# Cross-attention with 128 small heads: values of two head groups share a PSUM region, one copy and one pick per token tile, and the projections move to the stacks' bank

## The reference

```
q = Wq @ x + bq ; k = Wk @ c + bk ; v = Wv @ c + bv      # per batch entry, 128 x 256
q, k = rope(q), rope(k)                                  # first 4 channels of each head
scores = q k^T / sqrt(8) ; p = softmax(scores)           # 256 x 256 per head
out = p v ; result = Wo @ out + bo
x = x + tanh(gate) * result
```

## Time and profile before

| | us |
|---|---|
| median of 3 runs (lowest, highest) | 1466.29 (1465.21, 1469.73) |
| profiled execution, its own time | 1469.58 |
| its span | 1467.8 |
| span minus TensorE's busy time | 255.4 |
| this stage in the trace, from VectorE's first fill at 234.9 to the next stage's first transpose at 464.9 | 230 |

### The profile page before, as it was taken

One profiled execution on the slowest core, in us unless ns is written; L12 is line 12 of the kernel. 1 busy time (PEld: TensorE's weight loads), 2 busy tenths in 40 slices (PEclk: granted clock), 3 DMA queues, 4 the chain that ended last, 5 costly groups with the idle time before them and its releaser, 6 DMA issues.

```text
span 1467.8 us, 23344 instructions
## 1 busy us (share of the span) xinstructions
PE 1212.4 (83%) x8571; PEld 854.7 (58%) x8571; DVE 870.8 (59%) x1864; ACT 608.3 (41%) x1335; POOL 332.1 (23%) x261
## 2 busy tenths in 40 slices
PE   1573683888897399889999977999977999999986
PEld 1353462434344156578988744555546788888854
DVE  6677795677766465325555576333355676566476
ACT  2442341456553241235433332333323665565443
POOL 1312000111000200213121124454420332223222
PEclk9655796789887599999999989999997999999998
DMA  7100005200001311500000051111011000000010
GB/s 246 55 2 2 0 1 216 121 1 2 1 1 73 111 62 37 188 22 2 1 1 1 1 189 33 55 43 54 21 62 59 1 1 1 1 1 1 1 44 29
DMA packets 32162, 63.93 MB, mean 44 GB/s; under 512 B 5344, under 2 KB 23392, under 8 KB 30144
## 3 DMA queue, kind: packets, MB, share of 16 engines
q1 hardware_dynamic: 31296, 60.52, 11.7%
q0 software_dynamic: 768, 2.10, 0.4%
HBM read 54.88 MB, written 9.70 MB: 44 GB/s over the span
## 4 chain that ended last, share of the span: by engine, by line
PE 55%; DVE 15%; issue 12%; POOL 4%; ACT 3%; DMA 1%; DVEq 0%; SPq 0%; POOLq 0%; ACTq 0%
PE psum L1436 7%; PE psum L2494 4%; PE psum L2522 4%; PE psum L2484 4%; PE psum L1418 3%; PE psum L1742 3%; PE psum L2466 2%; PE psum L2448 2%; PE psum L1077 2%; PE psum L2820 2%; PE psum L2046 2%; PE psum L1103 2%; PE psum L1760 2%; PE psum L1045 1%; PE psum L1110 1%
## 5 line engine op out<-in xcount | busy, mean ns | idle before, releaser
L1169 ACT ACTIVATE c_probs<-psum 128x512 f32<-128x512 f32 x128 | 76.3, 598 | 67.2 <-PE psum L1088 67.2
L1273 DVE TENSOR_REDUCE c_max<-psum 128x2 f32<-128x512 f32 x128 | 84.5, 687 | 29.6 <-PE psum L1077 23.1
L1479 ACT ACTIVATE m_h_hi<-m_h 128x512 bf16<-128x512 f32 x50 | 31.5, 629 | 143.1 <-DVE m_h L1521 123.0
L1544 POOL TENSOR_TENSOR m_h_lo<-m_h,m_h_hi 128x512 bf16<-128x512 f32 x50 | 61.4, 1228 | 111.1 <-ACT m_h_hi L1479 111.0
L1436 PE MATMUL psum<-ctxT_yT_hi,m_w_hi 128*128 128x512 bf16 x200 | 78.0, 390 | 6.0 <-DVE m_h L1495 6.0
L1436 PE MATMUL psum<-ctxT_yT_hi,m_w_lo 128*128 128x512 bf16 x200 | 78.0, 390 | 0.0
L1516 DVE TENSOR_TENSOR m_silu_up<-psum,m_silu 128x512 f32<-128x512 f32 x44 | 30.4, 692 | 80.0 <-PE psum L1436 79.7
L1436 PE MATMUL psum<-ctxT_yT_lo,m_w_hi 128*128 128x512 bf16 x200 | 77.6, 388 | 0.0
L2522 PE MATMUL psum<-a_wo,a_outT 128*128 128x256 f32 x256 | 75.1, 405 | 0.7 <-DVE x_tok L2703 0.7
L2143 PE MATMUL psum<-a_wo,a_outT 128*128 128x256 f32 x256 | 75.2, 407 | 0.0
L1286 POOL TENSOR_TENSOR c_rope_terms<-c_rope_terms 128x256 f32<-128x256 f32 x16 | 11.7, 728 | 257.6 <-DVE c_rope_terms L1229 257.6
(11 more groups left out here) (495 smaller groups left out, 3474.3 us busy)
## 6 DMA issues: line engine op xcount, KB each, us to landing
m_w<-m_w SPq DMA_DIRECT2D x8, 1536.0 KB, 16.7
m_w<-m_w SPq DMA_DIRECT2D x27, 384.0 KB, 3.1
a_wq<-a_wq SPq DMA_DIRECT2D x2, 2048.0 KB
a_wo<-a_wo SPq DMA_DIRECT2D x2, 2048.0 KB, 12.0
a_trig<-trig_sin_cos SPq DMA_DIRECT2D x1, 2048.0 KB, 6.3
ctxT_yT_hi<-f_gate_up SPq DMA_DIRECT2D x2, 1024.0 KB, 7.4
a_sin_cos<-a_trig SPq DMA_DIRECT2D x1, 2048.0 KB, 9.7
m_rows<-m_zeros SPq DMA_DIRECT2D x1, 1920.0 KB, 13.4
```

Source lines behind the costliest of these rows:

```text
L1169: e.activation(c1P[:, n % 8, :, :], ps[:, 2 + n % 2, :].rearrange("p (k t) -> p k t", k=2), ACT.Exp, scale=float(1.0 / np.sqrt(np.float32( ...
L1273: e.tensor_reduce(c1M[:, u % 2, j, :], ps[:, c1_score_bank(n), :].rearrange("p (q t) -> p q t", q=2), AX.X, ALU.max).then_inc(c1_mx, 1)
L1544: e.tensor_tensor(hl[:, n_ % hb, :], hf[:, n_ % hb, :], hh[:, n_ % hb, :], ALU.subtract).then_inc(s_hl, 1)
```

## The change

For each pair of groups of a tile, values now accumulate into one PSUM region: head slots of one group have their 8 value columns at 0 to 7 and ones at 8 to 15, those of the other at 16 to 23 and 24 to 31, and zeros elsewhere. The order of groups within a tile becomes 0, 2, 1, 3, so that the two groups of a region have heads in different halves. A tile thus needs two regions of 256 columns, which fill bank 4, one ScalarE copy of 512 columns (r = 8 of the next tile), and one job of picks (r = 11), now eight matmuls, four for the numerators and four for the sums, both into bank 7. The four `sums` matmuls per tile and their counters are gone, with three of the four copies.

ScalarE then copies the picked rows (512 columns, `rows`), VectorE inverts the sums out of SBUF in two halves (r = 12 and 13), and the multiplication goes to GpSimd (`normalise`). The output projection moves from r = 14 to r = 3 of the next tile; ScalarE applies gate and bias to it (`gated`), and GpSimd adds it to `x` (`residual`). VectorE has neither any more.

The projections move to bank 6, which they share with the stacks, and to r = 4, 8 and 12. They have counters of their own (`c1_jobs_full`, `c1_jobs_read`). A job in bank 6 waits for the copy of the last stack, and a stack waits for the read of the last job. Bank 7 keeps the maxima, the picks and the output projection.

The fill of the value tile goes from VectorE to GpSimd (zeros, then two fills of ones). Four slots are added at the end, and the layernorm at the end covers six tiles first and the seventh last.

```diff
-            if i + 1 < NT and r in (3, 6, 10):
-                jobs.append(({3: "q", 6: "k", 10: "v"}[r], i + 1))
-            if i >= 1 and r in (11, 14):
-                jobs.append(({11: "num", 14: "wo"}[r], i - 1))
+            if i + 1 < NT and r in (4, 8, 12):
+                jobs.append(({4: "q", 8: "k", 12: "v"}[r], i + 1))
+            if i >= 1 and r == 11:
+                jobs.append(("num", i - 1))
+            if i >= 2 and r == 3:
+                jobs.append(("wo", i - 2))
...
+        def c1_bank6(e, what, idx):
+            n = c1_events[what, idx] - 1
+            if n:
+                e.wait_ge(c1_jobs_read, n)
+            if c1_stacked(what, idx):
+                e.wait_ge(c1_qk, c1_stacked(what, idx))
...
             def stacks(u):
...
+                e.wait_ge(c1_jobs_read, c1_before_stacks(u))
...
             def values(u):
...
-                if u:
-                    e.wait_ge(c1_ev, u)
...
+                region = slice(g // 2 * T1, (g // 2 + 1) * T1)
...
+                        ins = e.matmul(ps[32 * j:32 * j + 32, 4, region], c1v[:, i % 2, kt, 4 * C1_GROUP[g] + j, :], c1P[:, (4 * u + j) % 8, kt, :],
+                                       start=(g % 2 == 0 and kt == 0), stop=(g % 2 == 1 and kt == 1), skip_group_check=True, tile_position=(0, 32 * j))
...
-            def sums(u):
-                i, g = u // 4, u % 4
-                e.wait_ge(c1_ev, u + 1)
-                e.matmul(ps[32 * g:32 * g + 32, 4, T1:2 * T1], c1pick[:, 1, :], c1N[:, u % C1_NS, :], start=True, stop=True,
-                         skip_group_check=True, tile_position=(0, 32 * g)).then_inc(c1_sd, 1)
...
+                for what in range(2):
+                    for g in range(4):
+                        q = C1_GROUP[g]
+                        ins = e.matmul(ps[32 * q:32 * q + 32, 7, what * T1:(what + 1) * T1], c1pick[:, g % 2, what, :], c1N[:, g // 2, :],
+                                       start=True, stop=True, skip_group_check=True, tile_position=(0, 32 * q))
...
+            def outT(i):
+                e.wait_ge(c1_pv, 4 * i + 4)
...
+                e.activation(c1N[:, :, :], ps[:, 4, :].rearrange("p (r t) -> p r t", r=2), ACT.Copy).then_inc(c1_ev, 1)
...
+                e.activation(c1ND[:, :, :], ps[:, 7, :].rearrange("p (r t) -> p r t", r=2), ACT.Copy).then_inc(c1_read, 1)
...
+                e.activation(c1T[:, :], ps[:, 7, 0:T1], ACT.Identity, scale=gates[:, 1:2], bias=c1b[:, 5:6]).then_inc(c1_read, 1)
...
-            dve_step(e, e.memset(c1v[:, :, :, :, :], 1.0))
...
+                e.reciprocal(c1D[:, own], c1ND[:, 1, own]).then_inc(c1_iv, 1)
...
+                if n >= NH1 and n % NH1 in (12, 13):
+                    invert(n // NH1 - 1, n % NH1 - 12)
...
+                e.tensor_tensor(c1O[:, :], c1ND[:, 0, :], c1D[:, :], ALU.mult).then_inc(c1_dv, 1)
...
+                e.tensor_tensor(xt[:, i, :], xt[:, i, :], c1T[:, :], ALU.add).then_inc(c1_x, 1)
```

More of the change, by code:

```diff
@@ L1004, in c1_steps @@
                     yield "q4", c1_maxed(n)
-        c1_order = list(c1_steps())
-        for n, key in enumerate(c1_order):
-            c1_events[key] = n + 1
+        for own in (lambda what: what in C1_BANK6, lambda what: what not in C1_BANK6):
+            for n, key in enumerate(k for k in c1_steps() if own(k[0])):
+                c1_events[key] = n + 1
         def c1_score_bank(n):
@@ L1035, in project @@
             def project(what, i):
-                c1_bank7(e, what, i)
+                c1_bank6(e, what, i)
                 if what == "v":
                     for kt in range(2):
-                        ins = e.matmul(ps[:, 7, kt * P:(kt + 1) * P], ct[:, i, kt * P:(kt + 1) * P], c1w[:, 4, :], start=True, stop=True)
+                        ins = e.matmul(ps[:, 6, kt * P:(kt + 1) * P], ct[:, i, kt * P:(kt + 1) * P], c1w[:, 4, :], start=True, stop=True)
                 else:
@@ L1145, in c1_pe @@
                     values(c1_group(n, C1_PV))
-                if c1_group(n, C1_DEN) is not None:
-                    sums(c1_group(n, C1_DEN))
                 if j == 2 and u + 1 < U1:
@@ L1191, in c1_act @@
                     queries_with_max(c1_maxed(n))
-                if c1_group(n, C1_PV + 1) is not None:
-                    outT(c1_group(n, C1_PV + 1))
-                if n >= NH1 and n % NH1 == 9:
-                    sums(n // NH1 - 1)
+                for what, i in c1_jobs(n):
+                    if what == "num":
+                        rows(i)
+                    elif what == "wo":
+                        gated(i)
+                if n >= NH1 and n % NH1 == 8:
+                    outT(n // NH1 - 1)
                 if n % 4 == 2 and n // 4 + 1 < U1:
@@ L1264, in c1_dve @@
                 for what, i in c1_jobs(n):
[L1265 to L1269 removed]
+                    if what in ("q", "k", "v"):
                         project(what, i)
@@ L1295, in c1_pool @@
                         parts(what, i)
-            e.wait_ge(c1_hl, 2 * NT)
+                    elif what == "wo":
+                        residual(i)
+                if n >= NH1 and n % NH1 == 13:
+                    normalise(n // NH1 - 1)
+            e.wait_ge(c1_x, NT)
             finish(e, 4)
```

122 lines of the change are left out of this document (64 added, 58 removed).

## The result

In alternation on one chip the kernel before took 1468.0 us (median of 4, 1465.2 to 1473.1) and the changed kernel 1435.4 us (median of 4, 1429.8 to 1441.0): ratio 0.977, 95% interval 0.9741 to 0.9799. It is 32.6 us faster. The profiled executions, on which all readings of traces rest, are 28.6 us apart (spans 1467.8 and 1439.2). The changed kernel's is the longest of its four (1441.0).

The account below looks back on a forecast made before the run. TensorE and VectorE wait for each other by turns. Laps -11.2, start -1.8, end +1.7, few laps before it -0.5: -11.8 us, so 1457.8 for the profiled execution and 1454.5 from the median 1466.3; range 1440 to 1463.

Parts of the forecast that it names:

- The step that failed: Middle tiles: TensorE's longest wait, 1.78 us now, was estimated at 1.75 one lap later; clock loss unchanged, counted as nothing.
- Rival (a): Seven tiles: clock stays up because the wait comes in two pieces; the 10.7 us lost come back, 1444 us; chance 0.24.
- The plain lap: L1065 to next L1065 without projection (last tile): 4.25 us loses its 0.55 us `sums` matmul, giving 3.70, set by TensorE.
- The r = 1 lap: Stretch from r = 1 to the next L1065, with output projection (0.63) and q (1.07): 5.40 us against 5.51.
- The r = 9 lap: Stretch from r = 9 to the next L1065, with picks (1.00) and v (0.71), without the inversion: 5.41 us against 7.11.
- The r = 13 lap: Stretch from r = 13 to the next L1065, set by VectorE: its pieces sum to 6.06, lap about 5.45 us against 4.68.
- The start: Ahead of the first projection: the fill of the values moves from VectorE to GpSimd, gaining 1.76 us.
- The end: Serial stretch from the last `values` to the next stage's first transpose: 8.1 us against 6.4, a loss of 1.7 us.
- the laps without maxima: The few laps just before the serial end lose their `sums` too but are set by exponentials: 0.5 us gained.
- GpSimd's part: Multiplication and residual move to GpSimd at about 0.73 us each, covered by its idle time and the later output projection.
- rival (b): GpSimd contention stretches VectorE by 3 us and a fuller ScalarE keeps each lap 0.2 us longer: 1463 us; chance 0.15.
- Rival (c): Bank 6: stacks wait for VectorE's projection reads; 1.0 us late at each of 21 stacks gives 1475 us; chance 0.06.

## Why the prediction was right or wrong

**What bounds the kernel.** That TensorE and VectorE wait for each other by turns held, and so did the places: the longest wait is now before the L1093 that follows r = 13, three laps are TensorE's and one is VectorE's.

**The step that failed** is this one: "The longest wait keeps its length, so I let the clock fall as often as now and count nothing for it." It doesn't keep its length. The wait of 1.78 us became 0.60 and 0.79 with matmuls between, 1.39 in all, since maxima stand between inversion and columns (with the inversion in one piece it is the same). Each fall of the clock now costs less too: 1.5 us more for its tile, instead of 1.5 to 3.4, 2.6 on average. On the six middle tiles this is 6.9 us in the profiled executions. That it is the shorter waits which spare the clock is argued and not isolated: with the product back on VectorE the scores wait 1.36 us, and the clock falls in two of six tiles. Rival (a), the clock stays up, was the nearer case and had the right reason in it ("it comes in two pieces"); but it isn't that the clock stays up altogether: it falls in one to four tiles of six. Its price was also too low. The 10.7 us count seven middle tiles of 22.6, but the seventh window has no projections and is 19.4 at full clock (4.68 + 4.25 + 4.25 + 6.24), so the loss was 13.8, and (a) would have said 1441.

The clock is not the larger part. The profiled execution, 1440.9, lies 16.9 us below the 1457.8 forecast for it: the tiles at full clock make 8.2 of this (19.4 for 11.2), the clock 6.9, the start 2.9, the rest of the program, by chance, 2.4, and the end takes 3.4 off.

**The terms that were mis-sized**, in the laps all in one direction. By lap, forecast and measured at full clock: r = 1, 5.40 and 4.76; r = 5, 4.77 and 4.48; r = 9, 5.41 and 5.34; r = 13, 5.45 and 5.05. Sum 21.0 and 19.63, so the gain of a tile is 3.0 instead of 1.6 us; over six middle tiles 17.9 instead of 9.6.
- The plain lap: 3.70 forecast, 3.41 measured. The matmul was sized rightly (0.56 by the added one). Taking out the sums' matmuls alone gives 3.65; the other 0.24 appears only where one 512-column copy serves two groups and this lap has none. That this copy is the reason is argued, not isolated.
- The r = 1 lap: I added both projections at full length from the chain, q at 1.07, to a plain lap that was too long. The measured lap is 1.35 above the plain one, of 1.70.
- The r = 9 lap came out near by luck: the plain lap was 0.29 too long, and picks and v were 0.22 too short (1.93 measured, 1.71 forecast).
- The r = 13 lap: the pieces are the right ones, but I summed durations where starts count, since VectorE starts an instruction before the one ahead has ended. From the read of v (396.99) to L1093 (402.48) it is 5.49 us for my 6.06: the halves of the inversion stand 0.86 and 0.85 from their successors instead of 0.95 (the first starts at 398.35 and its maximum at 399.21), the four maxima 2.4 together instead of 2.76. TensorE's L1093 comes 0.44 after v's read, where I had 0.6 from v's end.

**The start**: 2.5 us instead of 1.76, within the scatter; up to the first L1093 of r = 1 it is 4.65, in which the clock of the first tile's laps has a part. **The end**: 8.8 us instead of 8.1, because I took the picks at full clock (1.1 forecast, 1.97 measured). I counted a gain of 0.5 for the laps without maxima ahead of it; they lost 2.3 (from 7.1 to 9.4), at low clock and with an output projection among them. Together the end costs 4.65 us where I had 1.2.

**GpSimd's part** was right in price (0.724 and 0.722 us for 0.73), and the cover held. Moved back, the two cost 10.7 us, which I had counted inside the laps without a price of its own: 5.4 of it is the product, ahead of a maximum in the one lap that VectorE sets. I had also credited the laps with the 7.1 us that L1247 waits; moved alone, the residual is worth nothing.

**Contention, rival (b)**, didn't come but went: L1281 takes 194 to 196 ns in all 32, with more work on GpSimd, and the stretches that the earlier trace rows has are gone. I had priced only what two more GpSimd instructions would add, and not what the new slots would take away. The Trainium skill (GPSIMD Engine Reference, Specifications) has the two engines share their SBUF interfaces, with contention where VectorE's instruction has two SBUF inputs. The traces agree. Beside the new product on GpSimd there are 14 maxima, which read PSUM, and they take 626 to 678 ns, no more than others. At the end an instruction of the layernorm with two SBUF inputs (L163) meets L1321 and takes 0.73 us instead of 0.17; nothing waits for it. **Rival (c)** didn't come either: no stack (L1083) waits for VectorE's reads. Sharing that bank is, on the contrary, part of the shorter tile, since no L1065 then waits for a read of bank 7, as it does in the run with the slots alone.

**Which part of the change brings what.** By ratios to the kernel before: slots alone 0.8%, with the bank 1.2%, with the sums' matmuls 1.8%, all of it 2.35%. The sums alone are 0.2%, and 0.6% once the banks are apart. Each ratio is known to 0.2 to 0.4%, so neighbouring steps are not all clear of each other; slots against nothing, and all of it against the banks alone, are. The parts do not seem to add: each is worth what the lap that it shortens lets through.

**What stays open** is what exactly makes the clock fall. With bank and slots TensorE idles 1.8 us of a tile of 21.36, and the clock stays up; in the changed kernel it idles 1.6 of 19.63, and the clock falls in some tiles. So idle time by itself doesn't tell the two apart. The pieces lie differently (0.71 and 0.41 as the longest in the one, a lap apart, 0.60 and 0.79 within one lap in the other). With the added matmul and with the inversion spread, where the clock stayed up too, the 0.60 is gone and one piece of 0.79 or 0.77 is left. But no run varies that alone, and each of these is one or two executions.

## What to carry to other kernels

Where two engines wait for each other by turns, first find the lap that each sets: work taken from an engine counts only in its own laps, and an edit that only reorders the other engine's queue can be worth more than one that removes work. A wait that gets shorter, or is split by work between, can also change TensorE's granted clock, so put a price on it from rows at both levels, for each way, instead of counting the clock as unchanged. The end of such a stage is serial, and its clock can change with the laps ahead of it (0.90 before, 0.50 with the change): price it at both levels too. And look for instructions stretched beside another engine's in the old order: a reordering can take such a cost away.

## What the runs showed of the hardware that was not expected

- Added work can pay for itself in part: one more 256-column matmul per group made the laps 9.3 us longer in all and cost 5.3 us, with the granted clock at 1.00 over the seven tiles, where three traces without it have 0.93, 0.97 and 0.93. The other way round, with the sums' matmuls out and the banks apart, the one trace has low clock in four of six middle tiles (0.71 in the lap shown), where the one with the sums left in has none.
- The three projections in other slots and nothing else shortened the tile by 0.5 us and were worth 12 us; in the traces most of it came through the clock (low in one of six middle tiles instead of five).
- A VectorE instruction with two SBUF inputs of 128x8, 0.194 us alone, took 0.433 or some 0.62 us beside GpSimd's instructions, 13 times of 32.
- ScalarE's copy with scale and bias from per-partition columns, 256 columns out of PSUM, takes 0.56 us (L1210), against 0.38 for a plain one of the same shape (L1177 in the kernel before).
